# A decoder layer on one core: constant rows built in place, less bias traffic, a new order of the first stage, one norm shared by two engines

## The chip, the core and the metric

The kernel runs on one core of a Trainium2 chip. TensorE (PE) multiplies, VectorE (DVE), ScalarE (ACT) and GpSimd (POOL) work on vectors, and SyncE (SP) issues the transfers. Each engine takes its own instructions in order; semaphores tie them together. The metric is the device time of one execution in microseconds, lower is better.

## What is computed

x has 16 sequences of 256 tokens with 128 features, the context 16 sequences of 64 tokens. Three blocks follow each other, each with a norm ahead of it:

```python
x = x + attn(layernorm(x))            # 16 heads of 8, causal softmax, layernorm(qkv)*gamma+beta, Wo
x = x + xattn(ctx, ctx, layernorm(x)) # one head of 128, 64 keys per sequence, biases bv, bq, bo
x = x + ffn(layernorm(x))             # 8 experts 128 -> 512 -> 128, relu, gates by 1.5-entmax over 8 logits
```

Every expert is computed for every token and weighted by its gate. All of it is in 32-bit floats.

## The kernel before

**Tiling.** The tokens go in 8 pairs of sequences: 512 tokens, four tiles of 128. A product is made of three, with both operands split in a high and a low part (`three`, L1038 to L1040): ScalarE writes the high part from PSUM, VectorE the low part, which it gets by subtraction. A tile of stacked rows (`stacks`, or `qs0` and `ks0` for pair 0) holds for every head 32 rows: high and low parts of q and k, put there by six transfers of 256 KB (`stack_rows`, L725 and L730), the rows of the maxima (`nm_rows`, L738), and constant rows that carry a part of the causal mask.

**Phases.** `run_phases` runs phase 0 (`FIRST`: all weights are loaded, transposed, split and folded; pairs 0 and 1 go through attention), then eight rounds. A round has 32 chunks of the experts for pair f, beside them the attention and cross attention of pair f+1 (`A_STEPS`) and the projections and maxima of pair f+2 (`Z_STEPS`), and closes pair f-1. In the lists every step has its place on each engine as a number (`pe=`, `act=`, `dve=`, `pool=`, `sp=`): an engine takes its steps by rising number, so the lists are the order, written out by hand. `FILL` gives how many matmuls without a use (L1079) go ahead of a step of phase 0.

**Steps by name.** SZ and NZ are the first norm (statistics on VectorE L1589 and L1592, four small instructions on GpSimd L909 to L914, scaling on ScalarE L1404), T1 transposes, Q, K and V project. MAX (24 in phase 0, L1104, L1112, L1657) finds the row maxima, MT transposes them, SC makes scores (L1132), exponentials on ScalarE (L1462) and the mask on GpSimd (L902). PV is probabilities times values, BT brings it back, SA, NA and TA, T2, T3 are the three later norms and their transposes: 0 to 2 are those of pair 0, 3 to 5 those of pair 1 in phase 0. In the rounds T3 (SA 2, NA 2) gives `fT_hi` and `fT_lo`, which the first product of the next round needs. XS, PT, XO are the cross attention, `xwv`, `cT`, `kp`, `w1` and others are tables made from weights and context. w1L and w2L load experts' weights, w1r and w2 split them: ScalarE the high part, GpSimd the low part. The step w1 (n) multiplies them anew and needs the GpSimd parts of w1r up to n // 2.

**The front of phase 0.** SyncE issues 17 loads (L706 to L716, four of them single vectors of 512 bytes), then w1L 0 and 1, XL, bL (the bias rows of the experts, spread over all partitions: 512 KB written), RL, then `spread_cells`: eight transfers (L747) that put the constant rows in the stacks of pair 0, from two small tiles that GpSimd makes in `cells` (L885 to L893). Behind them on the same queue stand the six transfers of K 0. Before its own `cells`, GpSimd fills both stacks of pair 0 (L868, L869), and in `masks` those of pair 1 (L872, L873). The first MAX on TensorE waits for all of these.

Of the kernel before, what the change touches and what calls it, by code (L numbers as in the profile page):

```python
# [23 lines left out]
ALU = mybir.AluOpType  # L24
# [3 lines left out]
P = 128  # L28
# [37 lines left out]
class Step(NamedTuple):  # L66
# [100 lines left out]
    Step("stacks", 0, "-", pool=0.25),  # L167
    Step("w1L", 0, "-", sp=0),
    Step("w1L", 1, "-", sp=0.25),
    Step("NZ", 0, "-", act=0),  # L170
    Step("XL", 1, "-", sp=0.5),
    Step("bL", 0, "-", sp=0.75),
    Step("xwq", 0, "-", dve=0.25),
    Step("RL", 0, "-", sp=1),
    Step("T1", 0, "u", pe=0, act=0.25, dve=0.5),
    Step("cells", 0, "-", pool=0.5, sp=1.25),
    Step("Q", 0, "y", pe=0.25, act=0.75, dve=0.75),
    Step("masks", 0, "-", pool=0.75),
    Step("w1r", 0, "-", act=0.5, pool=1),
    Step("K", 0, "m", pe=0.5, act=1, dve=1, sp=1.5),  # L180
    Step("xwv", 0, "u", pe=0.75, act=1.5, dve=1.5),
    Step("w1r", 1, "-", act=1.25, pool=1.75),
    Step("cT", 0, "v", pe=1, act=1.75, dve=1.25),
    Step("V", 0, "t", pe=1.25, dve=2.75),
    Step("pairs", 0, "-", act=2, dve=2.25),
    Step("w1L", 2, "-", sp=1.75),
    Step("SZ", 1, "-", dve=1.75, pool=1.25),
    Step("w1L", 3, "-", sp=2),
    Step("xwk", 0, "m", pe=1.5, act=2.25, dve=2),
    Step("w2L", 0, "-", sp=2.25),  # L190
    Step("vp", 0, "v", pe=1.75, act=2.75, dve=2.5),
    Step("constants", 0, "-", pool=1.5),
    Step("xwo", 0, "m", pe=2, act=2.5, dve=3),
    Step("kp", 0, "y", pe=2.25, act=3, dve=3.25),
    Step("cT", 1, "s", pe=2.5, act=3.25, dve=3.5),
    Step("MAX", 0, "h", pe=2.75, dve=3.75),
    Step("w1r", 2, "-", act=3.5, pool=2),
    Step("wo", 0, "y", pe=3.25, act=3.75),
    Step("MAX", 1, "t", pe=3, dve=4),
    Step("MAX", 2, "h", pe=3.5, dve=4.25),  # L200
    Step("ka", 0, "m", pe=4, act=4, dve=4.75),
    Step("w1", 1, "y", pe=4.25, act=4.75, dve=5.5),
    Step("MAX", 3, "s", pe=3.75, dve=4.5),
    Step("NZ", 1, "-", act=4.25),
    Step("MAX", 4, "h", pe=4.5, dve=5.25),
    Step("w1r", 3, "-", act=4.5, pool=2.25),
    Step("MAX", 5, "t", pe=4.75, dve=5),
    Step("T1", 1, "m", pe=5, act=5, dve=6.5),
    Step("MAX", 8, "t", pe=5.25, dve=5.75),
    Step("MT", 0, "v", pe=5.75, dve=6.25, sp=2.5),  # L210
    Step("vo", 0, "y", pe=6, act=5.25, dve=7.5),
    Step("MAX", 9, "s", pe=5.5, dve=6),
    Step("MAX", 6, "t", pe=6.25, dve=6.75),
    Step("bias", 0, "m", pe=6.75, act=5.5),
    Step("cells", 1, "-", sp=2.75),
    Step("MAX", 7, "s", pe=6.5, dve=7),
    Step("MAX", 10, "t", pe=7, dve=7.25),
    Step("Q", 1, "m", pe=7.5, act=5.75, dve=8),
    Step("MAX", 11, "h", pe=7.25, dve=7.75),
    Step("SC", 0, "t", pe=7.75, act=6, pool=2.5),  # L220
    Step("wr", 0, "y", pe=8.25, act=6.5, dve=8.25),
    Step("SC", 1, "s", pe=8, act=6.25, pool=2.75),
    Step("vp", 1, "v", pe=8.5, act=6.75, dve=9),
    Step("SC", 2, "t", pe=8.75, act=7, pool=3),
    Step("MT", 1, "y", pe=9.25, dve=8.5, sp=3),
    Step("w1", 5, "m", pe=9.5, act=7.5, dve=9.25),
    Step("SC", 3, "s", pe=9, act=7.25, pool=3.25),
    Step("gwo", 0, "u", pe=9.75, dve=8.75),
    Step("SC", 4, "s", pe=10, act=7.75, pool=3.5),
    Step("K", 1, "m", pe=11.25, act=9, dve=9.5, sp=3.25),  # L230
    Step("PV", 0, "y", pe=10.5, act=8.75),
    Step("SC", 5, "t", pe=10.25, act=8, pool=3.75),
    Step("SC", 6, "s", pe=10.75, act=8.25, pool=4),
    Step("w1", 2, "t", pe=11.5, act=9.25, dve=9.75),
    Step("SC", 7, "h", pe=11, act=8.5, pool=4.25),
    Step("SC", 8, "s", pe=11.75, act=9.5, pool=4.5),
# [60 lines left out]
    Step("ka", 1, "m", pe=23.75, act=18.25, dve=20),
    Step("SA", 2, "-", dve=19.5, pool=8.75),
    Step("SC", 17, "s", pe=23, act=18, pool=8.5),
    Step("SC", 18, "h", pe=24, act=18.5, pool=9),  # L300
    Step("XO", 1, "y", pe=24.5, dve=20.25),
    Step("SC", 19, "t", pe=24.25, act=18.75, pool=9.25),
    Step("w2", 3, "-", act=19, pool=9.75),
    Step("V", 1, "v", pe=24.75, dve=20.75),
    Step("SA", 5, "-", dve=20.5, pool=9.5),
    Step("NA", 2, "-", act=19.25),
    Step("NA", 5, "-", act=19.5),
    Step("MT", 3, "s", pe=25, dve=21, sp=4.5),
    Step("T3", 0, "u", pe=25.25, act=19.75, dve=21.25),
    Step("T3", 1, "v", pe=25.5, act=20, dve=21.5),  # L310
]
# [101 lines left out]
def bass_decoder_layer(nc, x, ctx_in, wq, wk, wv, wo, gamma, beta, xwk, xwv, xbv, xwq, xbq, xwo, xbo,  # L413
# [6 lines left out]
    with ctx:  # L420
# [87 lines left out]
        br_row = x1[0:1, 2, E // 2:E // 2 + NE]  # L508
        acc = sb("acc", [P, TOK])

        cell_rows = acc[0:ROWS, :].rearrange("p (a s) -> p a s", a=2)
# [190 lines left out]
        def _(sp):  # L702
# [1110 lines left out]
```

## Time and profile before

| | us |
|---|---|
| median of 3 runs | 665.39 |
| lowest and highest | 664.62, 668.40 |
| the profiled execution | 664.33 |
| its span, first to last instruction | 662.6 |
| phase 0, to the first product of an expert | 100.16 |
| TensorE busy | 618.6 (93%) |
| VectorE, ScalarE, GpSimd busy | 464.3, 408.0, 363.9 |

The profile shows one execution. The timeline gives for a group of instructions its start, its length, and in brackets how long the engine had been idle before it and what released it. The chain follows back from the last instruction what each one waited for. The busy share of TensorE is overstated somewhat, since ends of matmuls are modelled. The phase without the experts is 15% of the span; the eight rounds are the rest.

### The profile page before, as it was taken

Reading aid. Unit: us, or ns where it says so; the run is one execution under the profiler, and the core shown is the slowest. Engines: PE = TensorE matmul, PEld = TensorE weight load, DVE = VectorE, ACT = ScalarE, POOL = GpSimd, SP = SyncE. Lnnn points to the kernel's source line nnn. Section 1 sums busy time; section 2 is a strip of 40 time slices with the busy share of each in tenths; the row PEclk is TensorE's granted clock in tenths of the full one; section 3 lists DMA queues with packets and bytes.
Section 4 is the critical chain, followed back from the end, with each engine's and each line's share of the span. In section 5 each row is a group of like instructions: output and inputs, shape, how many; then the busy total and the mean of one; then the engine's idle time right before and its main releaser. Section 6 shows DMA issues by size and latency. Waiting matters only on the chain.

```text
span 662.6 us, 15729 instructions
## 1 busy us (share of the span) xinstructions
PE 618.6 (93%) x5263; PEld 459.8 (69%) x5263; DVE 464.3 (70%) x996; ACT 408.0 (62%) x780; POOL 363.9 (55%) x599
## 2 busy tenths in 40 slices
PE   5488879999999999999999999999999999998997
PEld 3355557777677767777678767777677767776775
DVE  4495984679747986689747986599557984656544
ACT  4239476755777566755766557755776567665543
POOL 8625565445663737444763746544753756464363
PEclk9889999999999999999999999999999999999999
DMA  6705100530027000630036000720045000700230
GB/s 187 230 17 169 45 4 18 127 117 4 19 45 208 10 8 14 151 107 2 18 67 191 0 20 0 162 95 2 18 98 159 2 2 6 159 2 1 55 88 16
DMA packets 39195, 43.76 MB, mean 66 GB/s; under 512 B 2922, under 2 KB 23670, under 8 KB 39158
## 3 DMA queue, kind: packets, MB, share of 16 engines
q1 hardware_dynamic: 39158, 43.28, 24.5%
q8 instruction: 22, 0.36, 0.2%
q14 instruction: 15, 0.12, 0.1%
HBM read 10.04 MB, written 2.10 MB: 18 GB/s over the span
## 4 chain that ended last, share of the span: by engine, by line
PE 77%; DVE 8%; ACT 6%; POOL 3%; issue 2%; DMA 2%; SPq 2%; ACTq 0%; DVEq 0%; POOLq 0%
PE h_ps L1038 10%; PE y_ps L1038 9%; PE h_ps L1040 8%; PE h_ps L1039 8%; PE y_ps L1040 8%; PE y_ps L1039 8%; DVE negmax L1657 5%; PE sbuf_m L1149 5%; PE sbuf_s L1132 3%; PE sbuf_s L1104 2%; ACT prob L1462 2%; PE sbuf_s L1149 2%; PE sbuf_s L1053 1%; PE sbuf_s L1066 1%; PE sbuf_m L1038 1%
## 5 line engine op out<-in xcount | busy, mean ns | idle before, releaser
L1773 DVE SCALAR_TENSOR_TENSOR h_lo<-h_ps,h_hi 128x512 fp32r<-128x512 f32 x256 | 172.2, 682 | 120.3 <-ACT h_hi L1481 119.4
L1481 ACT ACTIVATE h_hi<-h_ps 128x512 fp32r<-128x512 f32 x256 | 152.1, 601 | 129.7 <-PE h_ps L1040 127.7
L1038 PE MATMUL h_ps<-fT_lo,w_hi 128*128 128x512 f32 x256 | 111.6, 436 | 4.1 <-DVE fT_lo L1626 2.7
L902 POOL TENSOR_SCALAR_AFFINE_SELECT prob<-prob 128x512 f32<-128x512 f32 x128 | 79.8, 642 | 60.7 <-ACT prob L1462 57.2
L1462 ACT ACTIVATE prob<-sbuf_s 128x768 f32<-128x768 f32 x124 | 95.2, 813 | 25.7 <-PE sbuf_s L1132 25.7
L1038 PE MATMUL y_ps<-h_lo,w_hi 128*128 128x512 f32 x255 | 106.9, 419 | 1.5 <-ACT y_sb L1490 1.5
L1657 DVE TENSOR_REDUCE negmax<-sbuf_s 128x4 f32<-128x1024 f32 (+1 forms) x91 | 106.9, 1212 | 0.1
L1039 PE MATMUL h_ps<-fT_hi,w_lo 128*128 128x512 f32 x256 | 101.2, 395 | 0.0
L1040 PE MATMUL h_ps<-fT_hi,w_hi 128*128 128x512 f32 x256 | 101.1, 395 | 0.0
L1040 PE MATMUL y_ps<-h_hi,w_hi 128*128 128x512 f32 x255 | 100.8, 395 | 0.0
L1039 PE MATMUL y_ps<-h_hi,w_lo 128*128 128x512 f32 x255 | 100.7, 395 | 0.0
L909 POOL TENSOR_TENSOR vareps_a<-mv_a,eps_t 128x4 f32<-128x4 f32 (+1 forms) x27 | 5.4, 200 | 157.5 <-DVE mv_a L1592 157.5
L983 POOL TENSOR_TENSOR y_sb<-y_sb,gate_b 128x512 f32<-128x512 f32 x55 | 70.9, 1290 | 11.9 <-ACT y_sb L1490 11.9
L986 POOL TENSOR_TENSOR acc<-acc,y_sb 128x512 f32<-128x512 f32 x55 | 70.7, 1286 | 4.3
L1038 PEld LDWEIGHTS h_ps<-fT_lo,w_hi 128*128 128x128 f32 x256 | 48.0, 188 | 19.9 <-DVE fT_lo L1626 4.0
L1038 PEld LDWEIGHTS y_ps<-h_lo,w_hi 128*128 128x128 f32 x255 | 47.9, 188 | 17.8 <-DVE h_lo L1773 3.5
L1040 PEld LDWEIGHTS h_ps<-fT_hi,w_hi 128*128 128x128 f32 x256 | 48.1, 188 | 11.5
L1040 PEld LDWEIGHTS y_ps<-h_hi,w_hi 128*128 128x128 f32 x255 | 47.9, 188 | 11.5
L1039 PEld LDWEIGHTS y_ps<-h_hi,w_lo 128*128 128x128 f32 x255 | 48.1, 188 | 7.6
L1490 ACT ACTIVATE y_sb<-y_ps,biasT 128x512 f32<-128x512 f32 x63 | 43.6, 691 | 15.5 <-PE y_ps L1040 13.1
L1039 PEld LDWEIGHTS h_ps<-fT_hi,w_lo 128*128 128x128 f32 x256 | 48.3, 189 | 6.3
L1149 PE MATMUL sbuf_m<-prob,v_t 128*32 128x128 f32 (+1 forms) x704 | 33.2, 329 | 0.0
(449 smaller groups left out, 1046.2 us busy)
## 6 DMA issues: line engine op xcount, KB each, us to landing
gate_b<-gT SPq DMA_DIRECT2D x64, 256.0 KB, 4.9
stacks<-qk SPq DMA_DIRECT2D x42, 256.0 KB, 2.5
gate_b<-in_L_ffn_W_dram SPq DMA_DIRECT2D x8, 512.0 KB, 6.1
x_r<-in_x_dram SPq DMA_DIRECT2D x8, 256.0 KB, 4.0
x_t<-in_x_dram SPq DMA_DIRECT2D x7, 256.0 KB, 2.7
out_dram<-sums SPq DMA_DIRECT2D x7, 256.0 KB, 4.4
w_hi<-qk SPq DMA_DIRECT2D x3, 256.0 KB, 4.5
w_lo<-qk SPq DMA_DIRECT2D x3, 256.0 KB, 5.4
```

The costliest lines, as they stand in the source:

```text
L902: pool.affine_select(out=v, in_=v, compare_op=ALU.is_ge, fill=0.0, base=0, pattern=[[0, 2], [0, 2], [1, P]], channel_multiplier=-1).then_i ...
L983: mark(pool.tensor_tensor(y, y, gate_b[:, e, :], ALU.mult))
L986: pool.tensor_tensor(acc[:, :], acc[:, :], y, ALU.add).then_inc(summed, 1)
L1038: pe.matmul(out_ap, w_hi, m_lo, start=start, stop=False)
L1039: pe.matmul(out_ap, w_lo, m_hi, start=False, stop=False)
L1040: return pe.matmul(out_ap, w_hi, m_hi, start=False, stop=stop)
L1149: last = pe.matmul(o[:, 0:S] if first else o[:, P:S], tile[:, c:c + VW], blocks(prob[:, (2 * n + v) % PG, j, :], first), start=first and v ...
L1462: act.activation(pair_of_heads(n), halves[buf][:, :, 0:3 * P], ACT.Exp).then_inc(free[buf], 1)
L1481: act.activation(h_hi[:, c % HB, :], h_ps[:, c % 2, :], ACT.Relu).then_inc(hhi_made, 1)
L1490: act.activation(y_sb[:, e % YB, :], y_ps[:, :], ACT.Identity, bias=biasT[:, e:e + 1]).then_inc(y_made, 1)
L1657: dve.tensor_reduce(negmax[:, tile, :].rearrange("p (j g) -> p j g", g=NG)[:, j:j + 2, gs], halves[buf].rearrange("p j (g s) -> p j g s", ...
L1773: dve.scalar_tensor_tensor(out=h_lo[:, c % HB, :], in0=h_ps[:, c % 2, :], scalar=0.0, in1=h_hi[:, c % HB, :], op0=ALU.max, op1=ALU.subtrac ...
```

## The change

1. The constant rows are no longer transferred. VectorE makes `cell_of` (the cell number of each column) and row numbers once, and writes a whole stack of 128x2048 with one `tensor_scalar` each for q and k, constants and zeros together (`stack_constants`). The four fills of GpSimd, its `cells` and the 16 transfers of `spread_cells` go. For pair 0 the two stand in SZ 0, around `setup`; for pair 1 they are the step stacks 1.
2. Bias rows: GpSimd clears 128x1024 once, and 2 transfers put 8 rows in place of the spread of 512 KB (with the spread vector `xbo`, 64 KB of writes that stay). "Parity" (`odd`) is multiplied in by ScalarE, and VectorE only adds.
3. The four single vectors are loaded from ScalarE's queue.
4. `level_xwq` uses `tensor_tensor` with a spread column for `tensor_scalar`, and is far later.
5. The order of phase 0 is new. SP: bL, XL 1, w1L 0, 3, 1, 2, K 0's stack rows, w2L 0, RL, w2L 2, K 1. VectorE: SZ 0, T1 0, xwv, SZ 1, Q 0, xwo, K 0, stacks 1, cT 0, xwk, T1 1, pairs, vp 0, wr, Q 1, MAX 1, MAX 0, K 1, MAX 4, 5, 2, 3, w1 7, w1 5, MT 0, and so on; V 0, cT 1, kp 0 come behind the first maxima, Q 1 and K 1 before or among them. TensorE: w1 5 stands ahead of MAX 4. GpSimd: masks, constants, SZ 1, then w1r 0 to 3.
6. Rounds: of the last norm ScalarE scales tiles 0 and 1, GpSimd tiles 2 and 3, right behind SA 2 and ahead of the next weighting of y.

```diff
@@ first stage, order (excerpt)
+    Step("K", 0, "t", pe=1, act=1.5, dve=1.5, sp=1.5),
+    Step("w1r", 0, "-", act=1.75, pool=1),
+    Step("stacks", 1, "-", dve=1.75),
+    Step("Q", 1, "m", pe=2.75, act=4.25, dve=3.5),
+    Step("MAX", 0, "h", pe=3, dve=4),
+    Step("K", 1, "y", pe=3.5, act=4.75, dve=4.25, sp=2.5),
+    Step("w1", 5, "m", pe=3.75, act=5, dve=5.75),
+    Step("MAX", 4, "t", pe=4, dve=4.5),
...
+    Step("w2", 3, "-", act=16.75, pool=7.75),
...
@@ SyncE
-            for n, v in enumerate([gamma, beta, xbv, xbq]):
-                sp.dma_start(vec_rows[n:n + 1, :], row(v)).then_inc(wq_loaded, 16)
...
-                    sp.dma_start(whole[:, 0:2 * F], b1.rearrange("(a n) f -> a (n f)", n=2).unsqueeze(1)
-                                 .to_broadcast([NE // 2, 32, 2 * F])).then_inc(b_loaded, 16)
+                    sp.wait_ge(whole_cleared, 1)
+                    for r in range(2):
+                        sp.dma_start(whole[r:P:32, 0:2 * F], b1.rearrange("(a n) f -> a (n f)", n=2)).then_inc(b_loaded, 16)
@@ GpSimd
+            pool.memset(whole[:, 0:2 * F], 0.0).then_inc(whole_cleared, 1)
...
-                pool.memset(words(qs0), 0.0).then_inc(const0_made, 1)
-                pool.memset(words(ks0), 1.0).then_inc(const0_made, 1)
...
+                    if n == 2 and not ph.first:
+                        pool.wait_ge(rstd_made["a"], ph.a * 3 + 3)
+                        pool.sem_inc(pool_turn, 1)
+                        for k in range(NT // 2, NT):
+                            ins = pool.tensor_scalar(ln[:, k, :], x2[:, k, :], rstd["a"][:, k:k + 1], drop["a"][:, k:k + 1],
+                                                     ALU.mult, ALU.add)
+                        ins.then_inc(normed_rest, 1)
@@ TensorE
+                    if name == "T3" and not ph.first:
+                        pe.wait_ge(normed_rest, ph.a)
@@ ScalarE
+                    for v in (b1_pairs, xbo_pair):
+                        act.activation(v, v, ACT.Identity, scale=odd[:, 0:1]).then_inc(pairs_hi, 1)
+                    ks = range(NT // 2) if n == 2 and not ph.first else ph.tiles(n // 3)
@@ VectorE
+                dve.wait_ge(cells_made, 4)
+                for k in which:
+                    dst, op, by = ((q_rows, ALU.is_equal, 1.0), (k_rows, ALU.is_gt, behind))[k]
+                    dve.tensor_scalar(dst[:, :, :].rearrange("p g (b s) -> p (g b) s", s=S), cells, row_at, by, op, ALU.mult)\
+                       .then_inc(stacks_made[n], 1)
...
+                        stack_constants(0, (0,))
                         setup()
+                        stack_constants(0, (1,))
```

## Rows read from the trace of the kernel before

**Rows 1.** The page: busy us of each engine, share, instructions.

```profile
PE 618.6 (93%) x5263; PEld 459.8 (69%) x5263; DVE 464.3 (70%) x996; ACT 408.0 (62%) x780; POOL 363.9 (55%) x599
```

**Rows 2.** Stretches: start:end, length, then busy us per engine, clock, DMA share, GB/s.

```profile
core 0: us, PE busy (x) PEld busy (x) DVE busy (x) ACT busy (x) POOL busy (x), PEclk, DMA share, GB/s
...
20.00:33.39 13.39, 4.95 (x44) 3.22 (x45) 4.65 (x9) 3.84 (x8) 7.04 (x17) 0.74 0.89 257
33.39:77.88 44.49, 39.24 (x541) 25.73 (x540) 34.84 (x57) 26.79 (x47) 18.52 (x23) 0.96 0.28 85
77.88:100.16 22.28, 16.48 (x161) 11.71 (x160) 19.34 (x48) 14.56 (x35) 15.56 (x27) 1.00 0.01 4
100.16:172.90 72.74, 71.68 (x634) 53.83 (x634) 53.53 (x118) 46.81 (x90) 37.18 (x64) 1.00 0.23 61
```

**Rows 3.** The chain of work, front of phase 0: start, us, what.

```profile
6.86 1.74 POOL w_hi L868
...
12.36 0.87 SPq L747
...
20.42 0.62 SPq L725
...
23.68 7.99 DMA w_lo<-qk
```

**Rows 4.** Timeline of VectorE: start, us, line, tiles [idle before <- releaser].

```profile
9.01 1.66 DVE L1542 TENSOR_SCALAR xwq_hi<-sums,tilt 128x128 fp32r<-128x128 f32 x1
...
10.76 0.29 DVE L1545 TENSOR_TENSOR xwq_lo<-sums,xwq_hi 128x128 fp32r<-128x128 f32 x1
10.97 0.68 DVE L1632 TENSOR_TENSOR tT_lo<-h_ps,tT_hi 128x512 fp32r<-128x512 f32 x1
...
15.30 0.69 DVE L1629 SCALAR_TENSOR_TENSOR qk<-sbuf_m,qk 128x512 fp32r<-128x512 f32 x1
...
23.68 1.28 DVE L1608 SCALAR_TENSOR_TENSOR w_lo<-w_lo,odd,prob 128x1024 fp32r<-128x1024 f32 x1
...
33.39 1.23 DVE L1657 TENSOR_REDUCE negmax<-h_ps 128x8 f32<-128x1024 f32 x1 [4.92 <-PE h_ps L1112]
...
36.79 1.23 DVE L1657 TENSOR_REDUCE negmax<-h_ps 128x4 f32<-128x1024 f32 x1 [1.04 <-PE h_ps L1112]
...
59.18 0.69 DVE L1629 SCALAR_TENSOR_TENSOR qk<-sbuf_m,qk 128x512 fp32r<-128x512 f32 x1 [2.95 <-ACT qk L1452]
...
66.89 0.69 DVE L1570 TENSOR_TENSOR w_lo<-y_ps,w_hi 128x512 fp32r<-128x512 f32 x1 [2.35 <-ACT w_hi L1389]
```

**Rows 5.** Timeline of GpSimd, front of phase 0.

```profile
8.53 1.81 POOL L869 MEMSET w_lo<- 128x2048 f32 x1
...
18.33 2.35 POOL L1008 TENSOR_TENSOR w_lo<-gate_b,w_hi 128x1024 fp32r<-128x1024 f32 x1
```

**Rows 6.** Issues of K 0 and later (L730): from issue to landing.

```profile
DMA to landing us min/median/max: 2.4/2.5/8.0
```

**Rows 7.** Timeline of TensorE: first product of an expert.

```profile
100.16 0.47 PE L1038 MATMUL h_ps<-fT_lo,w_hi 128*128 128x512 f32 x1 [1.08 <-POOL w_lo L1012]
```

**Rows 8.** Timeline, end of the second round.

```profile
241.86 0.20 POOL L914 TENSOR_TENSOR drop_a<-drop_a,rstd_a 128x4 f32<-128x4 f32 x1
...
242.70 1.64 ACT L1404 ACTIVATE ln<-sums,drop_a,rstd_a 128x128 f32<-128x128 f32 x4
...
244.07 0.39 PE L1205 MATMUL sbuf_s<-ident,negmax 128*16 128x128 f32 x2 [0.50 <-DVE negmax L1657]
244.39 0.42 PEld L1053 LDWEIGHTS sbuf_m<-ident,ln 128*128 128x128 f32 x4 [0.22 <-ACT ln L1404]
...
247.43 0.64 POOL L902 TENSOR_SCALAR_AFFINE_SELECT prob<-prob 128x512 f32<-128x512 f32 x1 [1.59 <-ACT prob L1462]
```

**Rows 9.** Timeline, end of the seventh round, the last with a norm.

```profile
605.39 0.63 PE L1053 MATMUL sbuf_m<-ident,ln 128*128 128x128 f32 x4 [0.91 <-ACT ln L1404]
```

**Rows 10.** Groups by line: GpSimd weights y with its gate.

```profile
L983 POOL TENSOR_TENSOR y_sb<-y_sb,gate_b 128x512 f32<-128x512 f32 x55 | 70.9, 1290 | 11.9 <-ACT y_sb L1490 11.9
```

More of the change, by code:

```diff
@@ L166 @@
     Step("SZ", 0, "-", dve=0, pool=0),
-    Step("stacks", 0, "-", pool=0.25),
-    Step("w1L", 0, "-", sp=0),
-    Step("w1L", 1, "-", sp=0.25),
+    Step("masks", 0, "-", pool=0.25),
+    Step("bL", 0, "-", sp=0),
     Step("NZ", 0, "-", act=0),
[L171 to L224, printed above, removed]
@@ L300 @@
[L300 to L305, printed above, removed]
+    Step("XL", 1, "-", sp=0.25),
+    Step("xwv", 0, "t", pe=0, act=0.25, dve=0.5),
+    Step("constants", 0, "-", pool=0.5),
+    Step("w1L", 0, "-", sp=0.5),
+    Step("xwo", 0, "m", pe=0.25, act=1, dve=1.25),
@@ new lines @@
+    Step("T1", 0, "v", pe=0.5, act=0.5, dve=0.25),
+    Step("w1L", 3, "-", sp=0.75),
+    Step("w1L", 1, "-", sp=1),
+    Step("Q", 0, "y", pe=0.75, act=1.25, dve=1),
+    Step("w1L", 2, "-", sp=1.25),
+    Step("pairs", 0, "-", act=0.75, dve=2.75),
+    Step("SZ", 1, "-", dve=0.75, pool=0.75),
+    Step("K", 0, "t", pe=1, act=1.5, dve=1.5, sp=1.5),
+    Step("cT", 0, "u", pe=1.25, act=2.25, dve=2),
+    Step("w1r", 0, "-", act=1.75, pool=1),
+    Step("NZ", 1, "-", act=2),
+    Step("stacks", 1, "-", dve=1.75),
@@ new lines @@
+    Step("xwk", 0, "m", pe=1.5, act=2.75, dve=2.25),
+    Step("T1", 1, "y", pe=1.75, act=3, dve=2.5),
+    Step("w1r", 1, "-", act=2.5, pool=1.25),
+    Step("bias", 0, "v", pe=2, act=3.25),
+    Step("vp", 0, "t", pe=2.25, act=3.75, dve=3),
+    Step("w2L", 0, "-", sp=1.75),
+    Step("w1r", 2, "-", act=3.5, pool=1.5),
+    Step("RL", 0, "-", sp=2),
+    Step("wr", 0, "y", pe=2.5, act=4, dve=3.25),
+    Step("Q", 1, "m", pe=2.75, act=4.25, dve=3.5),
+    Step("MAX", 0, "h", pe=3, dve=4),
+    Step("w1r", 3, "-", act=4.5, pool=1.75),
@@ L509, in bass_decoder_layer @@
         acc = sb("acc", [P, TOK])
-        cell_rows = acc[0:ROWS, :].rearrange("p (a s) -> p a s", a=2)
+        cell_of = acc[:, 0:S]
+        row_sums = acc[:, S:S + P]
+        row_at, behind, above, below_11 = (acc[:, S + P + k:S + P + k + 1] for k in range(4))
         gate_b = sb("gate_b", [P, NE, TOK])
@@ L565, in bass_decoder_layer @@
         const_made = sem("const_made")
-        const0_made = sem("const0_made")
+        stacks_made = [sem(f"stacks_made_{k}") for k in range(2)]
+        whole_cleared = sem("whole_cleared")
+        odd_made = sem("odd_made")
         filler_made = sem("filler_made")
@@ L589, in bass_decoder_layer @@
         nm_cleared = sem("nm_cleared")
+        cells_base = sem("cells_base")
+        rows_kept = sem("rows_kept")
         cells_made = sem("cells_made")
-        cells_loaded = [sem(f"cells_loaded_{k}") for k in range(2)]
         pool_turn = sem("pool_turn")
```

274 lines of the change are left out of this document (147 added, 127 removed).

## The prediction

> **What bounds the kernel now.** First the page's busy times: TensorE 93%, the next engine 70% [rows 1]. That is an average, so I read the stretches next [rows 2]. From 100.16 us on the experts run, and TensorE is busy 71.68 of 72.74 us there (98.5%): a round can only gain where TensorE stands still. Ahead of that lies phase 0 with 100.16 us. In 20 to 33.39 us every engine is at half or less (TensorE 4.95 of 13.39 us, granted clock 0.74) while the transfers are at 0.89; from 33.39 to 77.88 us VectorE is busy 34.84 of 44.49 us, then 19.34 of 22.28. So the front waits for transfers, and the rest is VectorE with gaps. The chain says which transfers [rows 3]: GpSimd's first fill at 6.86 and what follows it there, eight issues L747 on SyncE from 12.36 on, to 20.4, the six issues of K 0 behind them, and 7.99 us from the last of these to its landing at 31.67. The first maximum on VectorE starts at 33.39 after 4.92 us of idle time [rows 4].
>
> **Part 1, the front.** Removed from the chain are the fills and the eight issues. What is late next, K 0 or the constants? I walk VectorE in its new order. Statistics end near 5.0; five small instructions (0.2 to 0.3 each, as L1545's 0.29 for 128 columns) bring it to 6.2. One constant instruction has 2048 columns. No row has one: by L1608 (1024 columns in 1.28) and L1657 (1024 in 1.23) it is 2.3 us [rows 4]. First constant to 8.5, setup's 1.1 to 9.6, second to 11.9. T1's low part, at 10.97 before, starts there, 0.9 later; the low part of K, which ended at 15.99 (15.30 + 0.69 [rows 4]), ends at 16.9. ScalarE now has the four parity passes between T1 and Q, 2.7 us at the rate of its other passes, and ends them before Q arrives: no cost.
>
> SyncE: the issues take 0.6 each [rows 3]. Q's rows go at 15.7 to 17.5, K's to 19.3. Ahead of them in the transfer engines are 2 MB of w1 (0.5 MB each), gone 16 to 17 if they move at the 380 GB/s or so of the w1 loads; the clogging transfers of 48 KB and the 512 KB spread are not there. Landing then takes 2.5 us (the median of the other 23) to 8.0 (the one that stood in the queue) [rows 6]: 21.8 to 27.3. I take under 24, since what made it 8.0, w1L 2 and 3 and a backlog, is ahead of it or gone.
>
> VectorE after 16.9: stacks 1, 2 x 2.3, to 21.5; then cT, xwk, T1 1, pairs, vp, wr, Q 1 by rows of 0.69 for 512 columns and 1.28 for 1024, sum 4.3 net of overlap: 25.8. So **VectorE, not the transfers, is late next**, and the first maximum moves from 33.39 to 25.8: 7.6 us earlier. Bounds: 23.4 (constants at half price, then the landing decides) to 28.7 (landing at 27.3).
>
> The constants are a `tensor_scalar` on SBUF beside a busy GpSimd. L1542, 128 columns, took 1.66 us, and L1545, the same width as `tensor_tensor`, 0.29; the former lay beside the fill L869 and ended just after it (10.34) [rows 4, 5]. So such an instruction can be held for the rest of a GpSimd instruction, at most 2.35 us (L1008) [rows 5], and the value of 2.3 is kept between half and held. The Trainium skill ("SBUF — State Buffer", section "Who interferes with whom") states that: `tensor_scalar` in a two-port mode and any GpSimd instruction exclude each other, for whole instructions. By its page "VectorE: DVE Perf Modes" (the perf-mode tier table) 2048 columns would take 1.23 us; with that the sum would be 4.3 us less work on VectorE. This kernel's rows show the hold, not the double rate.
>
> **Part 2, from the first maximum to the first product.** Before: 33.39 to 100.16, 66.8 us. Added: `level_xwq` comes in here, 3 x 0.29 + 0.5 = 1.4. V 0, cT 1, kp 0 move in (2.1), T1 1, Q 1, wr move out (1.5): +0.6. Taken off: 1.0, the idle time at 36.79 [rows 4], which stands behind five filler matmuls at the low clock level (2.25 us of them). Filler falls from 50 to 42 in all, and TensorE idles less ahead of it. Then the gaps: VectorE is idle 9.65 us up to 77.88 and 2.94 after [rows 2]. Two large gaps, 2.95 and 2.35 [rows 4], lie at 56 to 67, where ScalarE has the exponentials of pair 0 and no maximum of pair 1 can run, as K 1's rows are only issued then. In the new order K 1 stands among the first maxima, so pair 1's maxima fill such gaps. I take half of the 5.3: -2.7. The moved w2 3 takes nothing off: it ends 1.08 us before the first product [rows 7], but T3's low part ends only 0.2 before it. Sum 66.8 + 1.4 + 0.6 - 1.0 - 2.7 = 65.1. First product at 25.8 + 65.1 = **90.9**, 9.3 us earlier. Unknown are the other gaps, about 7 us: none to twice.
>
> Where cover is thin: GpSimd's split of w1 (2.35 each [rows 5]) ends near 20, 22.4, 24.7 and 28 in my walk; w1 5 stands ahead of MAX 4 on TensorE and needs the third. It is due at about 27. Cover 2 us; if GpSimd is held longer, MAX 4 and everything behind it on TensorE wait.
>
> The loads of four vectors from ScalarE take 1.2 us off SyncE's issues; the norm's own chain (x loaded, SZ, GpSimd's root) sets T1, so nothing is gained. `level_xwq` without the hold and the lighter bias traffic are in the walk.
>
> **Part 3, the rounds.** SA 2's last result is there at 242.06 (241.86 + 0.20), ScalarE scales four tiles from 242.70 to 244.34, and T3's weights load 0.22 us later than they could; but just ahead of them TensorE had waited for the maxima until 244.07 [rows 8]. Six rounds look like this, five with this 0.22 (1.1 in all) and one with about 0.2. The seventh has no maxima, and the wait is 0.91 [rows 9]. With halves ScalarE ends 0.8 earlier. GpSimd's price for a tile: no row has it; 1.29 us for 512 columns of L983 [rows 10] gives 0.32 a tile, so two by 242.8, and even at 0.9 each they are done by 243.9, ahead of the maxima. Gain 1.1 + 0.2 + 0.9, less the next thing late: **2.0 us**. Behind it on GpSimd wait a weighting of y and two masks, 0.7 us later; GpSimd idled 1.59 us behind these, ahead of the next mask [rows 8], so they cost nothing.
>
> **Sum.** 664.33 - 9.3 - 2.0 = 653.0 for an execution like the profiled one, which lies 1.06 under the median of the runs. For the median: **654**.
>
> **Rivals.**
> 1. *The landing or the gaps.* The 2 MB ahead of K 0's rows make the last one land at 27.3 (the 8.0 of [rows 6]), and the first maximum starts at 28.7: +2.9. Or the gaps aren't filled (+2.7) and new ones come, since in-order engines must now meet at other places. Either gives 657, both 660. For it: the front's 2 MB; against: the transfers that moved slowly were the short ones.
> 2. *Constants at half price and full VectorE.* 1.15 us each: the walk ends at 23.4 instead of 25.8. And VectorE's gaps halve once more (-3.5). 654 - 2.4 - 3.5 = 648. The skill's double rate, named above, speaks for the first half; no row does.
> 3. *The front was not what counts.* If TensorE's and ScalarE's work behind the first maximum, and the chain of norms at the end (22.3 us from SA 3 to the first product [rows 2]), are fixed by ScalarE's exponentials, an earlier start turns into idle time: only the rounds' 2 us and a few more: 660.5 to 668. Against: VectorE is the one with the least slack in both stretches.
> 4. *Slower: constants and GpSimd in turns.* If each constant waits 2.35 for GpSimd and then holds it for 2.3, four times over, 9.4 us are added; w1r's third part comes at 34 instead of 24.7, TensorE stands at w1 5, and its clock falls as it did at 20 to 33 us (0.74), where ten us of its work take up to five more. 654 + 9.4 + 5 = 668. It needs more than 2.35 of hold per constant to reach the time before; L1542's hold was 1.4.
> 5. *The halves do not pay*: GpSimd takes over 1 us a tile, T3 waits for it: each 0.1 above costs 1.4 us over seven rounds. By L983 not likely; in the range.
>
> **How the numbers follow.** Forecast 0.55 (650.5 to 657.5), rival 1 0.19 (to 661), rival 2 0.14 (645 to 650.5), rival 3 0.08, rival 4 0.04. For 8 in 10 the range takes the forecast, rival 1 and the upper third of rival 2: 648.5 to 661. A measurement of this kernel tells about 0.5% (3.3 us) from no change. Faster than 662.1: forecast, rivals 1 and 2 and a bit of 3: 0.90. Within: 0.06. Slower: 0.04.
>
> **What would show it.** In the new profile: the first L1104 of TensorE at 22 to 26 us and VectorE's first maximum at 25.8; the landing of K 0's last rows before it; four `tensor_scalar` of 2048 columns on VectorE at 2.3 (or 1.2, or far more beside GpSimd); VectorE's idle time from there to the first product 8 to 11 us; the first product at 91; K 1 issued near 28; T3's wait for ScalarE gone in the rounds and a round 0.2 to 0.3 shorter, the seventh 0.9. Wrong would be: a first maximum after 29, TensorE waiting for GpSimd at w1 5, or a second half of phase 0 that is as much longer as the first is shorter.

## The result and the profile after

| | kernel before | kernel after |
|---|---|---|
| median of the runs, us | 667.72 (20 runs, 664.61 to 670.27) | 664.09 (20 runs, 662.29 to 669.74) |
| profiled execution, us (span, mean granted clock) | 664.33 (662.6, 0.991) | 664.98 (663.3, 0.979) |

The ratio of after to before is 0.9967, 95% interval 0.9952 to 0.9983 (the two medians alone would give 0.9946). The change makes the kernel 0.3% faster, within the half per cent that I called no change. I had forecast 654.

The two profiled executions must be compared with one thing in mind. That of before ran at a mean granted clock of 0.991, while the 40 timed runs of before in all the comparisons below had 0.979 to 0.989, and a line through them falls by 4.5 us for each 0.01 of clock (correlation -0.77). So the trace of before shows a good execution, and the two spans differ by +0.7 us where the medians differ by -3.6. Experiment 9 has the trace of a more usual one: it leaves phase 0 of before as it is, and there the clock does fall behind the first product.

The page of after (busy us, then the granted clock in tenths over 40 slices):

```profile
PE 623.7 (94%) x5246; PEld 464.1 (70%) x5255; DVE 475.9 (72%) x1014; ACT 403.6 (61%) x768; POOL 367.7 (55%) x606
...
PEclk9899957999999999999999999999999999999999
```

Beside [rows 1] TensorE has 17 instructions fewer and 5.1 us more of busy time: nearly the same matmuls took longer. The clock line says where: the sixth and seventh slice, 83 to 116 us. The stretches of after that answer to those of [rows 2], cut at its own first maximum (28.08) and first product (97.85):

```profile
20.00:28.08 8.08, 3.90 (x46) 2.84 (x47) 8.08 (x9) 3.50 (x7) 8.08 (x4) 1.00 0.58 179
28.08:77.88 49.80, 42.26 (x588) 29.45 (x593) 42.92 (x74) 26.03 (x44) 18.57 (x29) 0.97 0.21 65
77.88:97.85 19.97, 15.67 (x99) 11.25 (x99) 14.13 (x37) 11.90 (x30) 11.86 (x21) 0.62 0.03 9
97.85:173.80 75.95, 75.15 (x630) 56.39 (x630) 53.02 (x117) 45.50 (x87) 36.67 (x64) 0.94 0.21 56
```

The front did what the change is for: from 20 us to the first maximum VectorE is busy without a gap, where it had 4.65 us of work in 13.39 us. The granted clock of the last two rows was 1.00 in both in the trace of before, and is 0.62 and 0.94 now. The same place in fine slices:

```profile
70.00:80.00 10.00, 7.45 (x76) 5.50 (x68) 9.21 (x25) 4.22 (x9) 5.66 (x12) 1.00 0.02 5
80.00:82.00 2.00, 1.45 (x13) 0.83 (x18) 1.38 (x3) 1.56 (x5) 1.92 (x3) 1.00 0.00 0
82.00:84.00 2.00, 1.82 (x38) 1.65 (x34) 1.57 (x4) 0.34 (x2) 0.72 (x1) 0.69 0.03 8
84.00:94.00 10.00, 10.00 (x49) 7.96 (x48) 7.02 (x21) 6.03 (x16) 5.53 (x10) 0.50 0.00 0
94.00:96.00 2.00, 0.78 (x4) 0.32 (x3) 1.42 (x3) 2.00 (x6) 1.17 (x3) 0.50 0.00 0
96.00:106.00 10.00, 8.80 (x57) 6.38 (x58) 4.17 (x11) 2.65 (x6) 1.66 (x5) 0.50 0.11 32
106.00:108.00 2.00, 2.00 (x8) 1.55 (x8) 0.33 (x1) 1.64 (x3) 1.65 (x5) 0.83 0.00 0
```

TensorE runs at 0.50, its lower level of 1.2 GHz, from 84 to 106 us. What it did before the fall stands in its own timeline of after: three waits for the norms.

```profile
73.63 0.41 PE L1029 MATMUL sbuf_s<-ident,ln 128*128 128x128 f32 x2 [1.11 <-ACT ln L1384]
...
80.02 0.44 PE L1029 MATMUL h_ps<-ident,ln 128*128 128x128 f32 x2 [1.17 <-ACT ln L1384]
...
81.37 0.44 PE L1029 MATMUL y_ps<-ident,ln 128*128 128x128 f32 x2 [0.48 <-ACT ln L1384]
```

And what it costs, in the first products (TensorE's timeline of after): 0.63 us for a matmul and 0.42 from one to the next, where the trace of before has 0.39 and 0.23 (TensorE, 100.47 to 100.93 us).

```profile
97.85 0.77 PE L1014 MATMUL h_ps<-fT_lo,w_hi 128*128 128x512 f32 x1 [1.20 <-DVE fT_lo L1641]
98.42 0.63 PE L1015 MATMUL h_ps<-fT_hi,w_lo 128*128 128x512 f32 x1
98.84 0.63 PE L1016 MATMUL h_ps<-fT_hi,w_hi 128*128 128x512 f32 x1
```

The first product was at 100.16 [rows 7], so phase 0 is 2.3 us shorter, not 9.3. From the norm's last low part ahead of it to the same instruction a round later are 76.61 us (97.19 to 173.80) against 72.73 before (99.53 to 172.26). The account of the spans: front -2.3, first round +3.9, the other rounds -0.9, the last stretch +0.1: 0.7 longer, as measured. The +3.9 is against the good execution of before; against the trace of experiment 9, whose first round takes 75.66 us, it is +0.95.

The rounds of after, the end of the second as in [rows 8], and the seventh as in [rows 9]:

```profile
243.47 0.20 POOL L887 TENSOR_TENSOR drop_a<-drop_a,rstd_a 128x4 f32<-128x4 f32 x1
...
243.89 0.89 POOL L973 TENSOR_SCALAR ln<-sums,rstd_a,drop_a 128x128 f32<-128x128 f32 x2 [0.22 <-POOL drop_a L887]
...
244.33 0.87 ACT L1384 ACTIVATE ln<-sums,drop_a,rstd_a 128x128 f32<-128x128 f32 x2
...
245.70 0.39 PE L1183 MATMUL sbuf_s<-ident,negmax 128*16 128x128 f32 x2 [0.50 <-DVE negmax L1672]
...
245.96 0.42 PEld L1029 LDWEIGHTS sbuf_m<-ident,ln 128*128 128x128 f32 x4 [0.16 <-issue]
...
605.98 0.42 PEld L1029 LDWEIGHTS sbuf_m<-ident,ln 128*128 128x128 f32 x4 [0.51 <-issue]
```

GpSimd's two tiles end at 244.78, ScalarE's at 245.20, both ahead of TensorE's transposes of the maxima at 245.70. From these to the load of T3's weights it took 0.32 before (244.07 to 244.39) and takes 0.26 now. The five middle rounds are 73.53 us each where they were 73.56 (173.80 to 541.44 us, before 172.26 to 540.05). The seventh is 65.86 against 66.64.

VectorE at the front of after:

```profile
5.61 1.29 DVE L1531 TENSOR_SCALAR w_hi<-acc 128x2048 fp32r<-128x2048 f32 x1
...
7.83 2.21 DVE L1531 TENSOR_SCALAR w_lo<-acc 128x2048 fp32r<-128x2048 f32 x1
...
16.57 4.58 DVE L1531 TENSOR_SCALAR stacks<-acc 128x2048 fp32r<-128x2048 f32 x2
...
22.48 2.00 DVE L1617 TENSOR_TENSOR w_lo<-w_lo,prob 128x1024 fp32r<-128x1024 f32 x1
24.39 2.44 DVE L1617 TENSOR_TENSOR w_hi<-w_hi,prob 128x128 fp32r<-128x128 f32 x1
...
28.08 1.21 DVE L1672 TENSOR_REDUCE negmax<-sbuf_s 128x8 f32<-128x1024 f32 x1
```

and GpSimd beside it:

```profile
7.15 1.80 POOL L863 MEMSET v_t<- 128x2048 f32 x1
...
16.65 12.41 POOL L988 TENSOR_TENSOR w_lo<-gate_b,w_hi 128x1024 fp32r<-128x1024 f32 x4 [1.22 <-ACT w_hi L1407]
```

A constant of 2048 columns takes 1.29 us where GpSimd does only short work, and 2.21 where it began behind a fill of 1.80 us (7.15 to 8.95). The two at 16.57 took 1.28 and 3.39 beside the splits of w1, and those took 3.1 each in place of 2.35 [rows 5]. Then the two additions for the pairs took 2.00 and 2.44 us, the second for 128 columns, where 128 columns of such an addition took 0.29 [rows 4].

### The profile page after: what moved, and what is told of

It is laid out like the page before. It is cut to its first block, busy times and chain, and to the rows that moved or that the text cites. A ratio compares the mean times of both kernels' runs of the same rounds, so it can differ in the third digit from the quotient of the medians.

```text
span 663.3 us, 15713 instructions
## 1 busy us (share of the span) xinstructions
PE 623.7 (94%) x5246; PEld 464.1 (70%) x5255; DVE 475.9 (72%) x1014; ACT 403.6 (61%) x768; POOL 367.7 (55%) x606
## 4 chain that ended last, share of the span: by engine, by line
PE 77%; DVE 10%; ACT 6%; issue 3%; POOL 2%; DMA 1%; SPq 1%; ACTq 0%; DVEq 0%; POOLq 0%
PE h_ps L1014 10%; PE y_ps L1014 9%; PE h_ps L1015 8%; PE h_ps L1016 8%; PE y_ps L1016 8%; PE y_ps L1015 8%; PE sbuf_m L1125 5%; DVE negmax L1672 4%; PE sbuf_s L1108 3%; PE sbuf_s L1080 2%; ACT prob L1449 2%; PE sbuf_s L1125 2%; PE sbuf_s L1029 1%; PE sbuf_m L1014 1%; PE sbuf_m L1015 1%
## 5 line engine op out<-in xcount | busy, mean ns | idle before, releaser
L1449 ACT ACTIVATE prob<-sbuf_s 128x768 f32<-128x768 f32 x121 | 92.7, 812 | 29.6 <-PE sbuf_s L1108 29.6
L1672 DVE TENSOR_REDUCE negmax<-sbuf_s 128x4 f32<-128x1024 f32 (+1 forms) x89 | 104.9, 1215 | 2.6 <-PE sbuf_s L1088 2.5
```

The lines of the kernel that those rows point to most:

```text
L1449: act.activation(pair_of_heads(n), halves[buf][:, :, 0:3 * P], ACT.Exp).then_inc(free[buf], 1)
L1672: dve.tensor_reduce(negmax[:, tile, :].rearrange("p (j g) -> p j g", g=NG)[:, j:j + 2, gs], halves[buf].rearrange("p j (g s) -> p j g s", ...
```

## The experiments

The comparisons were made in three sets, each on another chip; before had medians of 667.9 (experiments 1 to 3 and 9), 668.1 (4, 6, 7, 10) and 667.4 us (5, 8) in them. Between two sets medians can be off by such a difference, so each ratio is that to before in the same set. I call a filler one of the 512-column matmuls of L1055 that keep TensorE running and compute nothing that is used.

**1. Fillers ahead of the late waits.** After's table of fillers, 17 more:

```diff
-FILL = {... ("T2", 0): 2, ("XS", 0): 1, ("T2", 1): 3, ("MT", 2): 1}
+FILL = {... ("T2", 0): 4, ("XS", 0): 1, ("T2", 1): 8, ("MT", 2): 1, ("TA", 1): 5, ("T3", 1): 5}
```

> The changed kernel with 17 filler matmuls more, put where TensorE waits late in phase 0 (5 ahead of TA 1, 5 more ahead of T2 1, 2 more ahead of T2 0, 5 ahead of T3 1). Theory clock: the changed kernel loses its gain because TensorE, idle at 72 to 82 us, is granted only 1.2 GHz from 82.7 to about 107 us. With the fillers the granted clock stays 1.0 there, the first product comes at 94 instead of 97.85, the first round takes 72.8 instead of 76.6 us, and the whole is 6 to 8 us faster than the changed kernel, 656 to 659. Rival work: the clock follows from something else and the fillers only cost their 0.21 us each where they overrun the wait: same time as the changed kernel, 664 to 665.

Measured: 658.85 us (657.31 to 659.14), ratio 0.9865 [0.9845, 0.9886], 5.2 under after's median (6.8 by the two ratios) with nothing but idle matmuls added. The time is the one expected; the first product was expected at 94 and came at 96.34. The windows of this kernel:

```profile
27.91:77.88 49.97, 43.50 (x593) 30.00 (x599) 42.95 (x75) 26.01 (x44) 18.59 (x29) 0.97 0.21 66
77.88:96.34 18.46, 14.89 (x110) 9.22 (x111) 14.08 (x36) 12.13 (x30) 11.76 (x21) 0.82 0.06 18
96.34:172.00 75.66, 74.53 (x664) 56.44 (x668) 54.69 (x120) 48.51 (x92) 40.03 (x69) 1.00 0.22 58
```

The first maximum is where it was (27.91), the first product 1.5 us earlier, and the first round is at 1.00. Its span of 657.4 lies 5.2 under that of before: 3.9 in phase 0 (the last low part starts at 95.66 against 99.53) and 1.3 in the rounds. Against after it is 1.5 in phase 0 and 4.0 in the first round (72.61 for 76.61). The clock still falls, to 0.57 from 88 to 96 us.

**2. The other direction:** the kernel before without its last 20 fillers (the expectation counts 21; the edit takes out 20).

```diff
-FILL = {... ("BT", 1): 1, ("T1", 1): 4, ("BT", 2): 1, ("TA", 0): 3, ("Q", 1): 3, ("V", 1): 1, ("TA", 1): 2, ("T2", 0): 2, ("WO", 1): 1, ("w1", 6): 2, ("w1", 7): 4, ("MT", 3): 4}
+FILL = {... ("BT", 1): 1, ("T1", 1): 4, ("Q", 1): 3}
```

> The kernel before without its 21 filler matmuls behind 73 us (ahead of BT 2, TA 0, V 1, TA 1, T2 0, WO 1, w1 6, w1 7, MT 3). Theory clock: the granted clock falls to 0.5 somewhere between 75 and 90 us and stays there into the first round, as in the changed kernel; the first product comes 1 to 3 us later and the first round is about 4 longer: 3 to 7 us slower than the kernel before, ratio 1.005 to 1.010. Rival work: fillers stand only in waits and are not needed: same time or 0.5 us faster.

Measured: 673.22 us (670.14 to 675.01), ratio 1.0084 [1.0059, 1.0109]. Its stretches:

```profile
80.00:84.00 4.00, 2.02 (x28) 1.20 (x29) 3.57 (x8) 1.75 (x4) 3.77 (x7) 0.50 0.00 0
...
100.00:110.00 10.00, 7.39 (x42) 5.36 (x46) 4.44 (x13) 2.73 (x7) 3.27 (x4) 0.50 0.10 30
```

5.3 us for taking away work that nobody waits for. The first product comes at 103.93, 3.8 us later, and the first round takes 77.15 for 72.73. With experiment 1 this shows it: in both orders some twenty fillers behind 70 us are worth 5 us, and the new order was laid with few of them there.

**3. The parts of the change in the order of before.** After's list `FIRST` and its fillers replaced by before's, less the steps that are gone, with the second set of constant rows just ahead of VectorE's first maximum:

```diff
+    Step("stacks", 1, "-", dve=3.6),
-    Step("stacks", 0, "-", pool=0.25),
-    Step("cells", 0, "-", pool=0.5, sp=1.25),
```

> All of the change except the new order: the changed kernel with the list of phase 0 and the fillers of the kernel before (steps stacks 0 and cells dropped, stacks 1 put just ahead of the first maxima on VectorE). Theory parts: the transfers and fills that are gone are what brings the first maximum forward, so it starts at 26 to 30 us instead of 33.4 and the clock, with the old fillers, stays up; 657 to 662. Theory order: without the new order the old places no longer meet, and the time is that of the kernel before, 664 to 668, or worse.

Measured: 661.49 us (659.34 to 662.43), ratio 0.9911 [0.9892, 0.9931]; 2.6 under the median of after, which has the same parts in its new order, and clear of it by the intervals. The theory of the parts holds (657 to 662), and the new order with its own fillers made the kernel slower. VectorE in it:

```profile
20.27 1.22 DVE L1617 TENSOR_TENSOR w_lo<-w_lo,prob 128x1024 fp32r<-128x1024 f32 x1
21.40 0.28 DVE L1617 TENSOR_TENSOR w_hi<-w_hi,prob 128x128 fp32r<-128x128 f32 x1
...
24.32 4.56 DVE L1531 TENSOR_SCALAR stacks<-acc 128x2048 fp32r<-128x2048 f32 x2
28.80 1.21 DVE L1672 TENSOR_REDUCE negmax<-h_ps 128x8 f32<-128x1024 f32 x1
```

The pairs' additions take 1.22 and 0.28 here, as GpSimd does only short instructions beside them (0.20 to 1.01 us). The constants take 4.56 beside its splits again, and now they stand ahead of a maximum whose scores TensorE had ready, so TensorE stands for 4.67 us until 30.06 and its clock is 0.67 in 30 to 40 us.

**4. The same with the constants one place later** (dve=4.6, behind four maxima).

> e2_old_order (old order and fillers) with stacks 1 moved behind MAX 3 on VectorE, since in e2_old_order it stood ahead of MAX 0 and TensorE waited 4.67 us for that maximum. Theory parts: the old order was right as it stood, and the first maximum now starts at about 24 us, 9 earlier than in the kernel before; 3 to 4.5 us faster than e2_old_order, 657 to 658.5. Rival: the 4.6 us are only moved, as VectorE is full to 77 us: within 1 us of e2_old_order.

Measured: 660.24 us (656.05 to 664.11), ratio 0.9876 [0.9839, 0.9913]. I had expected 657 to 658.5, or within 1 us of (3); 1.25 less is neither, and the two intervals overlap. First maximum at 24.74, 8.7 us ahead of before, constants 1.33 and 1.41; and yet the first product is at 98.42, later than in (3), where it is at 96.62. The clock is 0.54 from 30 to 52 us:

```profile
30.00:52.00 22.00, 18.84 (x142) 13.07 (x145) 15.65 (x19) 6.30 (x12) 4.65 (x3) 0.54 0.01 2
```

Its six runs lie in the order of their clock at both ends: 656.05 at 0.997, 664.11 at 0.979.

**5. That gap filled.** TensorE had waited 3.31 us for ka 0 there.

```diff
-FILL = {... ("MT", 3): 4}
+FILL = {... ("MT", 3): 4, ("ka", 0): 12}
```

> The changed kernel's parts (constant rows in place, the small parity rows, the halves) in the order and with the fillers of the kernel before, the second set of stack rows set late on VectorE, and 12 filler matmuls ahead of ka 0, where TensorE waited 3.31 us (29.3 to 32.6 us) in the same kernel without them and its granted clock then was 0.50 to 52 us. Clock theory: the granted clock of 30 to 52 us is near 1.00 again; there TensorE did 17 us of busy time at half clock, of which only what waits on TensorE counts, so the first product comes 2 to 4 us before 98.4 us and the median is 656 to 658 us (660.2 without). Rival, that the low clock of that stretch lies beside VectorE's work (8.99 busy of 10 at 30 to 40 us) and costs nothing: the clock rises, the first product stays at 97.5 to 98.5, the median 660 to 661. Second rival, that removing one gap only moves the fall of the clock to the next gap: the clock falls in another stretch before 100 us, median 659 to 661.

Measured: 659.14 us (657.58 to 660.44), ratio 0.9864 [0.9837, 0.9891]. First product 95.74, 2.7 us earlier, as the clock theory said; the medians are 1.1 us apart, which the intervals do not separate. The stretches:

```profile
30.00:52.00 22.00, 18.48 (x252) 12.21 (x253) 18.26 (x26) 13.66 (x25) 7.47 (x9) 1.00 0.11 39
70.00:90.00 20.00, 17.47 (x141) 12.78 (x140) 16.26 (x40) 11.07 (x28) 10.27 (x19) 0.74 0.01 2
96.00:98.00 2.00, 2.00 (x5) 1.52 (x5) 0.00 (x0) 0.60 (x1) 0.00 (x0) 0.50 0.46 133
```

1.00 where it was 0.54, but now 0.74 from 70 to 90 us, and 0.50 in the first products. The median is that of the second rival, which had the fall move on; both were right in part.

**6. After with its fillers (1) and the constants later**, at dve=5.1 in place of 1.75.

```diff
-    Step("stacks", 1, "-", dve=1.75),
+    Step("stacks", 1, "-", dve=5.1),
```

> e1_fill with one step moved: the constants of pair 1 (stacks 1, two instructions) go from just behind K 0, where GpSimd subtracts w1 in a row from 16.6 to 29 us, to behind the fourth maximum on VectorE, where GpSimd is idle. Theory hold: one of the two took 3.39 us for 1.28 as it was held by GpSimd's subtraction. In the new place both take 1.28, so 2.1 us of VectorE go; the two additions of the bias rows (2.00 and 2.44 for 1.22 and 0.28) stay held or shift; the first maximum starts 2 to 4 us earlier (24 to 26), and the whole is 1.5 to 3 us faster than e1_fill, 656 to 657.5. Rival rate: 2.3 us is their own time; then they take that in the new place too, and the time stays within 0.5 us of e1_fill.

Measured: 661.97 us (660.54 to 664.15), ratio 0.9913 [0.9886, 0.9940]. VectorE in this kernel:

```profile
20.72 2.24 DVE L1617 TENSOR_TENSOR w_lo<-w_lo,prob 128x1024 fp32r<-128x1024 f32 x1
22.89 2.45 DVE L1617 TENSOR_TENSOR w_hi<-w_hi,prob 128x128 fp32r<-128x128 f32 x1
...
26.59 1.21 DVE L1672 TENSOR_REDUCE negmax<-sbuf_s 128x8 f32<-128x1024 f32 x1
...
33.47 2.54 DVE L1531 TENSOR_SCALAR stacks<-acc 128x2048 fp32r<-128x2048 f32 x2
```

With GpSimd idle from 28 us the two constants take 2.54 together instead of 4.58, which shows the hold; the first maximum comes 1.3 us sooner, where I had expected 2 to 4. The kernel is 3.1 slower than (1) all the same: TensorE's clock is 0.80, 0.86 and 0.83 in 30 to 40, 40 to 50 and 70 to 80 us, against 0.97, 1.00 and 1.00 in (1), and the first product comes at 98.44. I had expected 656 to 657.5. The clock need not be the whole of it: from the first maximum to the first product it takes 71.85 us for 68.43 in (1), 3.4 more, and VectorE is busy 59.26 us there for 57.03, 2.2 more, as the constants now stand behind the first maximum. That a lower clock took the remaining 1.2 is likely, not shown.

**7 and 8. More fillers,** ahead of PT 1 (4) and ka 1 (3) on top of (6), and ahead of PT 0 (4) and ka 1 (2) on top of (1).

```diff
+("PT", 1): 4, ("ka", 1): 3
```

> f1_stacks_late with 7 fillers more, 4 ahead of PT 1 and 3 ahead of ka 1. In e1_fill the clock was granted at 1.2 GHz from about 88.7 to 95 us, after waits of 0.88 and 0.95 us there. Theory clock: it stays at 1.0 to the first product, which comes 1 us earlier: 0.5 to 1.5 us faster than f1_stacks_late. Rival: the seven fillers stand on the path in a stretch where every engine waits for the next one in the chain of norms: 0 to 1.5 us slower.

```diff
+("PT", 0): 4, ("ka", 1): 2
```

> The changed kernel with its 17 added fillers (658.85 us median) and six more: 4 ahead of PT 0 (TensorE idle 0.88 us there) and 2 ahead of ka 1. In the kernel with 17 the granted clock was 0.67, 0.50, 0.50 and 0.62 from 88 to 96 us, where TensorE was busy 6.0 us of 8; the first product came at 96.34 us. Clock theory: with the clock at 1.00 there, the three products and the transposes ahead of the first product (some 4.5 us of TensorE on the chain) take 1 to 1.5 us less, first product at 94.9 to 95.5, median 657.3 to 658. Rival, that the chain there runs over ScalarE, GpSimd and VectorE and six fillers only stand in its way: first product at 96.3 to 97, median 658.8 to 660.

Measured: 663.27 us (661.44 to 664.48) for (7), whose windows are

```profile
80.00:100.00 20.00, 16.39 (x125) 10.79 (x127) 14.35 (x37) 13.01 (x32) 11.70 (x20) 0.96 0.06 18
100.00:110.00 10.00, 10.00 (x74) 7.27 (x74) 4.10 (x10) 4.61 (x8) 3.46 (x10) 0.74 0.00 0
```

and 662.19 (658.54 to 665.73) for (8), 3.3 above (1). In (8) the first product is at 96.03 and the clock 1.00 from 88 to 96 us, as meant; but it is 0.62 from 84 to 88, and 0.66 and 0.50 from 96 to 100 and 100 to 104. Both are misses of what I expected from the clock. (7) was to be 0.5 to 1.5 us faster than (6) and is 1.3 slower, as its rival said, though the intervals overlap: (6) has 1.00 from 80 us to the end of its first round, and (7) 0.80 from 96 to 100, 0.50 from 100 to 104 and 0.85 from 104 to 108. Its first product is 0.95 us earlier, its first round 75.74 us for 72.57. (8) was to be at 657.3 to 658, by its rival at 658.8 to 660, and is above both: its first round takes 75.68 us for the 72.61 of (1). In both the fall lies in the first round, where TensorE is the bound and all of it counts.

**9 and 10. The halves,** on the kernel before alone, and taken out of (1):

```diff
+for k in range(NT // 2, NT):
+    ins = pool.tensor_scalar(ln[:, k, :], x2[:, k, :], rstd["a"][:, k:k + 1], drop["a"][:, k:k + 1], ALU.mult, ALU.add)
```

> The kernel before with nothing but the last norm of the rounds shared by ScalarE and GpSimd. Forecast of the prediction: 2.0 us faster. What the two traces say: the middle rounds were held by the maxima's transposes just ahead, not by ScalarE, so only 0.05 a round and 0.8 in the seventh: 0.9 to 1.2 us faster, ratio 0.998.

> e1_fill with the last norm of the rounds on ScalarE alone, as before. By the traces of both kernels the halves bring 0.05 us in each middle round and 0.8 in the seventh: 0.9 to 1.2 us slower than e1_fill. By the prediction 2.0 slower. By e3_halves_only against the kernel before 2.3 slower, whose clocks differed.

Measured: 665.57 us (663.71 to 668.69) for before with halves, ratio 0.9967 [0.9947, 0.9986]: 2.3 less. 660.18 (659.97 to 661.55) for (1) without them: 1.3 more than (1), with intervals that overlap (0.9882 [0.9858, 0.9906] against that of (1)). The traces give 1.5 between these two (505.83 us from the low part ahead of the first product to that of the last round in (1), 507.33 without halves): 0.2 in the first round, 0.4 in the five middle ones, 0.9 in the seventh. For before with and without halves they give 1.3 behind the first round; the rest of the 2.3 is within what the clock does from run to run.

The trace of (9) shows more. Up to the first product this kernel is before, with all 50 fillers, and its clock falls all the same:

```profile
90.00:100.00 10.00, 7.34 (x60) 5.58 (x60) 7.88 (x25) 8.17 (x19) 6.65 (x13) 1.00 0.00 2
100.00:105.00 5.00, 4.23 (x26) 3.45 (x30) 2.50 (x7) 1.30 (x3) 0.52 (x1) 0.70 0.20 59
105.00:110.00 5.00, 5.00 (x44) 3.54 (x37) 1.65 (x5) 2.11 (x3) 2.75 (x8) 0.62 0.00 0
```

Its first round takes 75.66 us (100.14 to 175.80) for the 72.73 in the trace of before. Its mean clock is 0.987, and 0.979 to 0.989 was that of the 40 runs of before. So a usual execution of before most likely pays some 3 us in its first round too (this is the one trace of it), and against that one the first round of after is only 0.95 us longer.

## Why the prediction was wrong

**What bounds the kernel:** right, but for GpSimd, which at 7.04 of 13.39 us in the front was above the half that I wrote. The transfers were ahead of the front's last wait, VectorE is late next, and the experts' rounds gain only where TensorE stands still.

**The walk along VectorE (25.8, measured 28.08).** K's low part was to end at 16.9 and ended at 16.6; the constants were to end at 21.5 and ended at 21.15. The price of 2.3 was right only as the mean of the last two: it is 1.28 unheld and up to 3.39 held, so both the double rate that I had left aside and the hold are real. What I left out is the hold on everything else. I had priced the pairs' additions by [rows 4], and they took 4.4 us where the same two take 1.5 unheld (experiment 3), since four splits of w1 stand on GpSimd without a gap from 16.65 to 29.06. That is 2.9 us, more than the whole miss of 2.3. The page "SBUF — State Buffer" of the Trainium skill, section "Who interferes with whom", names this case too: an operation of VectorE with two inputs in SBUF contends with a GpSimd instruction that reads SBUF; I had read it for the constants alone. The trace agrees: 2.44 us beside a split, 0.28 in experiment 3 beside short work.

**Landing of K 0's rows:** right in size; issue to landing took 3.0 and 3.2 us, and nobody waited for it. GpSimd's third split before MAX 4: the cover held, with 0.57 us of idle time on VectorE at 31.59.

**From first maximum to first product (65.1, measured 69.8; before 66.8).** This is the step that failed most, with 4.7 us: the gaps that were to be filled were not, and I took the clock as given. VectorE's busy time from one to the other is 57.05 us against 54.18 before, +2.9, where I had added 2.0. Its idle time is 12.7 us against 12.6: the 2.7 us of gaps that K 1's early place was to fill, and the 1.0 at 36.79, came back as other gaps. And the clock: I wrote that fillers fall from 50 to 42 and that TensorE "idles less ahead of it", and saw no cost in that. Nothing in the trace of before said that. Before has 20 fillers behind 73 us, which experiment 2 prices at 5.3 us with the first round, and the new table has few of them there. Of the 4.7 us experiment 1 gives back 1.3, with the clock (68.43 for 69.77 us). Of the other 3.4, 0.9 is work that I had not counted; why the gaps did not close is not shown. I had named as a sign of being wrong a second half that is as much longer as the first is shorter; the first is 5.3 shorter and the second 3.0 longer.

**The first round (forecast unchanged, measured +3.9).** I took its 72.74 us as given by the work. It is that at a granted clock of 1.00, and 75.95 at 0.94. Experiment 1 gives it back: 4.0 us in the traces. But most of the +3.9 is no loss against a usual execution of before, which has 75.66 there (experiment 9): it is a price that both kernels seem to pay in most runs, and that goes only with a clock held at 1.00.

**The rounds (2.0, measured 0.9 in the trace of after behind the first round, 1.5 in the traces of experiment 10, 1.3 and 2.3 in the medians).** GpSimd's tile took 0.45 us, not 0.32, and as said it did not matter. The seventh round gave 0.78 for my 0.9, in experiment 10 0.88. Of the 1.1 of the five middle rounds 0.15 was there, in experiment 10 0.4: [rows 8] show a wait of 0.22 behind the transposes of the maxima, and I should have asked how early the load could have been. These transposes ended next to it, so the wait took the place of an interval that stays without it: 0.32 before, 0.26 after, and 0.03 less in a round (0.08 in experiment 10).

**From execution to median.** I took the profiled execution as 1.06 us under the median, from three runs. Its clock of 0.991 lies above that of all 40 timed runs of before, and its time is 3.6 us under their median. From before's median of 20 runs, 667.72, my gain of 11.3 would have given 656.4: that is 2.4 of the 10.1 us between forecast and result. The other 7.7 are the gain that was missing, 3.6 for 11.3. The front's 2.3, the second stretch's 4.7 and 0.7 in the rounds (1.3 for 2.0) make these 7.7, with no share of the first round; the sum is mine, and of a usual execution of before there is only the trace of experiment 9 to bear it out.

**The rivals.** The range of rival 3 holds the result, for another reason than it gave: the earlier start turned into gaps on VectorE, more work there and a slower TensorE, and nothing shows ScalarE's exponentials as what fixed it. The clock stood in rival 4, but in the front, at w1 5. What I had no rival for is a fall of the clock at the end of the phase, which [rows 2] let one ask: TensorE stands still 5.8 us of 22.28 there. In the two traces the terms that failed are 2.3 + 4.7 + 3.9 + 1.1 = 12.0 us, against 12.0 between the span that I had forecast for an execution like the profiled one (662.6 - 11.3 = 651.3) and that of after (663.3). This sum has the good clock of the trace of before in it, by which the loss is 4.3 larger than in the medians.

**What stays open.** Experiments 5, 7 and 8 each filled a gap, and the clock then fell at another place. Which idle time lets it fall can't be said from these traces, and no kernel here kept it at 1.00 from 30 us to the second round, so the price of the remaining falls is not measured. The fastest single run, 656.05 at 0.997, suggests that some 3 us are left. The fastest versions are (1) with 658.85 us and (5) with 659.14, which their intervals do not separate: 0.986 of before, where the change as it stands has 0.997. (3), (4), (6), (7) and (10) are clear of both kernels too.

## What to carry to other kernels

Work that nobody waits for can be load that holds the clock: before an order is laid anew, list the filler matmuls by their place, and price the TensorE-bound stretch behind each at both levels of the clock. When a step is placed on VectorE beside a long instruction of GpSimd, price every VectorE instruction in that stretch as held, not only the new one. Before a sum is built on one trace, put its mean clock beside those of the timed runs: here the trace of before was better than every one of 40. And of a wait that is to be removed, look at what ends just ahead of it: if the engine was busy until then, the wait may be worth nothing.

## What the runs showed of the hardware that I had not expected

- A fall of the clock moves. TensorE ran at 0.50 from 84 to 106 us in after, at 0.57 from 88 to 96 in (1), at 0.54 from 30 to 52 in (4), and at 0.50 from 100 to 104 in (7) and (8), with much the same work and the order or the fillers changed. It also differs between executions: with one and the same phase 0 the trace of before has 1.00 from 100 to 110 us, that of (9) 0.70 and 0.62.
- Two runs of one kernel differ in clock: 0.979 to 0.997 in (4), with 8 us between them; lines through the runs of each kernel here give 2.2 to 4.8 us for 0.01 of mean clock.
- GpSimd is held as well: its `TENSOR_TENSOR` of 1024 columns took 3.1 us on average beside VectorE's constants and additions, 2.35 alone, and even a reciprocal root of 1.02 us took 1.52 beside the first constant:

```profile
5.42 1.52 POOL L885 TENSOR_TENSOR rstd_z<-vareps_z,minus_half 128x4 f32<-128x4 f32 x1
...
14.13 1.02 POOL L885 TENSOR_TENSOR rstd_z<-vareps_z,minus_half 128x4 f32<-128x4 f32 x1
```
